# Weights of layer 1's first groups prepared in other steps of a two-layer attention kernel

## What is computed

```python
x = x + tanh(g_xattn[0]) * L0_xattn(layernorm(x), ctx)   # 32 heads of 128, 8 key/value heads, q and k rms-normed
x = x + tanh(g_ffn[0])   * L0_ffn(layernorm(x))          # 8 LoRA experts of rank 16, softmax router
x = x + tanh(g_xattn[1]) * L1_xattn(layernorm(x), ctx)   # 16 heads of 96, 4 key/value heads
x = x + tanh(g_ffn[1])   * L1_ffn(layernorm(x))          # gated, inner width 1792
```

## Time and profile before

| what | us |
|---|---|
| median of 3 runs | 1165.22 |
| lowest and highest | 1164.53, 1165.63 |
| the profiled execution: its time | 1165.63 |
| its span in the trace | 1163.8 |
| PE busy | 1124.8 (97%) |
| DVE busy | 853.7 (73%) |
| ACT busy | 824.6 (71%) |
| mean granted TensorE clock | 0.994 of full speed |

### The profile page before, as it was taken

One profiled execution on the slowest core, in us unless ns is written; L12 is line 12 of the kernel. 1 busy time (PEld: TensorE's weight loads), 2 busy tenths in 40 slices (PEclk: granted clock), 3 DMA queues, 4 the chain that ended last, 5 costly groups with the idle time before them and its releaser, 6 DMA issues.

```text
span 1163.8 us, 22722 instructions
## 1 busy us (share of the span) xinstructions
PE 1124.8 (97%) x7184; PEld 707.8 (61%) x7184; DVE 853.7 (73%) x2066; ACT 824.6 (71%) x2695; POOL 373.6 (32%) x668
## 2 busy tenths in 40 slices
PE   8799999999999999999999999899999999899998
PEld 5456666666666666666656566566666765455554
DVE  5778777667767767677778889898888878743444
ACT  6978888888888888887778867777777765422221
POOL 5754434337533333433345443221111111100000
PEclk8999999999999999999999999999999999999999
DMA  7655654555654656464446566779987795100000
GB/s 255 158 126 113 138 140 120 123 110 110 145 132 91 151 132 139 116 118 106 96 101 139 129 114 131 154 136 186 226 179 138 145 179 103 42 1 1 37 1 37
DMA packets 411992, 139.56 MB, mean 120 GB/s; under 512 B 386656, under 2 KB 396640, under 8 KB 411872
## 3 DMA queue, kind: packets, MB, share of 16 engines
q1 hardware_dynamic: 409968, 134.43, 52.8%
q0 software_dynamic: 1904, 3.67, 1.2%
HBM read 39.21 MB, written 2.10 MB: 35 GB/s over the span
## 4 chain that ended last, share of the span: by engine, by line
PE 77%; DVE 12%; ACT 4%; issue 4%; POOL 3%; DMA 0%; DVEq 0%; POOLq 0%; ACTq 0%
PE bank L541 22%; PE bank L542 21%; PE bank L543 21%; PE bank L740 8%; PE bank L759 4%; DVE pieces L1108 2%; DVE mx L1211 2%; ACT probs L930 1%; DVE stats L1119 1%; POOL rstd L1514 1%; DVE x L1246 1%; DVE q_rows L1108 1%; ACT junk L837 1%; DVE oT L1108 1%; ACT pieces L834 1%
## 5 line engine op out<-in xcount | busy, mean ns | idle before, releaser
L834 ACT ACTIVATE pieces<-probs,rs 128x256 f16<-128x256 f32 x384 | 166.3, 521 | 11.8 <-DVE rs L1226 9.6
L1108 DVE SCALAR_TENSOR_TENSOR pieces<-probs,rs,pieces 128x256 f16<-128x256 f32 x384 | 164.6, 488 | 6.5 <-ACT pieces L834 5.4
L930 ACT ACTIVATE probs<-bank,nb,rq 128x256 f32<-128x256 f32 x256 | 141.3, 564 | 35.3 <-DVE nb L1216 34.9
L1211 DVE TENSOR_REDUCE mx<-bank 128x2 f32<-128x512 f32 x192 | 131.5, 685 | 45.4 <-PE bank L543 45.0
L837 ACT ACTIVATE junk<-bank 128x128 bf16<-128x128 f32 x384 | 101.7, 288 | 55.9 <-PE bank L543 55.9
L541 PE MATMUL bank<-wq,xT 128*128 128x512 f16 (+1 forms) x352 | 127.4, 362 | 3.4 <-DVE q_rows L1108 3.4
L541 PE MATMUL bank<-wo,oT 128*128 128x512 f16 x320 | 121.8, 381 | 6.4 <-DVE oT L1108 4.9
L542 PE MATMUL bank<-wq,xT 128*128 128x512 f16 (+1 forms) x352 | 127.3, 362 | 0.0
L543 PE MATMUL bank<-wq,xT 128*128 128x512 f16 (+1 forms) x352 | 127.1, 361 | 0.0
L543 PE MATMUL bank<-wo,oT 128*128 128x512 f16 x320 | 121.8, 381 | 0.0
L542 PE MATMUL bank<-wo,oT 128*128 128x512 f16 x320 | 121.8, 381 | 0.0
(11 more groups left out here) (216 smaller groups left out, 2841.7 us busy)
## 6 DMA issues: line engine op xcount, KB each, us to landing
raw_o<-in_wo_a SPq DMA_DIRECT2D x8, 1024.0 KB, 6.2
raw_q<-in_wq_a SPq DMA_DIRECT2D x7, 1024.0 KB, 6.1
raw_kv<-in_wkv_a SPq DMA_DIRECT2D x8, 512.0 KB, 3.8
turned<-pieces SPq DMA_TRANSPOSE x192, 2.8
raw_q<-in_wq_c SPq DMA_DIRECT2D x4, 768.0 KB, 4.9
raw_o<-in_wo_c SPq DMA_DIRECT2D x4, 768.0 KB, 5.0
down_rest<-in_down_t POOLq DMA_DIRECT2D x5, 512.0 KB, 4.2
ff_in<-in_gate_t SPq DMA_DIRECT2D x4, 448.0 KB, 4.0
```

What stands on the lines that cost most here:

```text
L834: return act.activation(out, in_, ACT.Copy, scale=scale)
L930: act.activation(probs[:, h, :], bank[h // 2][:, (h % 2) * KV:(h % 2 + 1) * KV], ACT.Exp, bias=nb[:, h:h + 1], scale=scale, accum_out=sums ...
L1108: return dve.scalar_tensor_tensor(out, in_, scale, hi, ALU.mult, ALU.subtract)
L1211: dve.tensor_reduce(mx[:, pr], chunks(bank[i][:, :], 2), AX.X, ALU.max, negate=True).then_inc(mx_done, 1)
```

## The change

Eight rows of three groups join the table of exceptions. Nothing else is changed, and no instruction is added or dropped.

```diff
         ("o", 7): (44, 46, 47, (48, 48, 49, 49)),
+        ("kv", 8): (45, 47, 48, (50, 50)), ("q", 8): (46, 48, 49, (50, 51, 51, 52)), ("o", 8): (50, 52, 53, (54, 55, 56)),
+        ("kv", 9): (58, 64, 65, (66, 67)), ("q", 9): (61, 65, 66, (67, 67, 68, 68)), ("o", 9): (64, 67, 68, (69, 70, 71)),
+        ("kv", 10): (68, 70, 71, (72, 73)), ("q", 10): (70, 71, 72, (73, 74, 75, 76)),
```

## The result

| | before | after |
|---|---|---|
| median of 12 runs each (us) | 1164.43 | 1168.78 |
| lowest and highest | 1162.02, 1167.16 | 1167.17, 1171.36 |
| span of the profiled execution | 1163.8 | 1168.0 |
| mean granted TensorE clock | 0.994 | 0.992 |

The changed kernel takes 1.0038 of the time before, with an interval of 1.0031 to 1.0046: slower by 0.4%, more than the 0.2% that can be told from no change. The forecast was 1167.5 us, and 2.3 us slower than before; it became 4.3 us slower, inside the range of 1162.0 to 1171.0. The forecast lay on the bound of 2.3 us; the measured change lies clear of it.

What follows compares the result with a forecast made beforehand. PE was taken to bound the kernel, with DVE setting the pace in the LoRA stretch. A 3.9 us gain from DVE's relief and a 6.2 us loss from the late q load gave 1167.5 us, range 1162.0 to 1171.0.

Steps and rivals of the forecast that it cites:

- Chunks out of steps 57 to 65: Ten q, o and kv chunks leave these DVE steps: 5.7 us less for DVE between two row maxima.
- the 4 us named as a sign: Sign of being right: PE's waits from 647 us to group 8's end shrink by about 4 us.
- Chunks into 50 to 52 and 54 to 56: Chunks added to DVE: 0.5 us late entering the LoRA tiles, and 0.9 us charged in full in 54 to 56.
- The squares in ACT's steps 47 and 48: Squares moved into these ACT steps have cover from free time and are costed at nothing.
- Steps 66 to 68: Exchanged chunks give DVE 0.9 us more; half counted, 0.4 us. Gain up to step 70: 3.9 us.
- The q load in step 70: Group 10's late load: ACT stands 8 us, PE 4.5 us, slower clock costs 1.7 us; loss 6.2 us.
- The kv load of group 10: Load moves from step 66 to 68, squares from 68 to 70: costs nothing, at most 0.5 us.
- The sum: Profiled 1165.63 - 3.9 + 6.2 = 1167.9 us; median 1165.22 + 2.3 = 1167.5 us.
- SP falls behind: Rival: after ACT's wait SP starts step 71's last transposes too late; loss 8, gain 3, 1170.2 us; chance 0.18.
- A load that isn't felt: Rival: the late q load causes no PE wait in step 72, leaving DVE's relief, 1161.3 us; chance 0.10.
- All idle time gone: Rival: DVE's relief removes all 6.7 us of PE's idle time in the LoRA stretch, 1164.7 us; chance 0.12.

Runs made afterwards that it cites:

- The stand-ins: Kernels with each DMA transpose replaced by two plain DMAs of half its size: the kernel before so edited 1164.42 us, the changed kernel 1168.34 us.
- the load back in step 69: Changed kernel with plain DMAs for transposes, and group 10's q load returned from step 70 to 69: 1163.28 us.
- The run with later squares: Changed kernel with plain DMAs for transposes, q load still in step 70, its squares moved from step 71 to 72: 1162.76 us.
- the stand-in of the change: Changed kernel with each DMA transpose replaced by two plain DMAs of half its size: 1168.34 us.
- the load alone: Kernel before, with plain DMAs for transposes and only group 10's q load moved to step 70: 1173.33 us.

## Why the prediction was right, and where it was not

**Chunks out of steps 57 to 65** (5.7 us). Right, a little large. DVE's stretch shrank by 5.0 us, and DVE did set the pace for most of it. Near the end it no longer does: two waits for PE's scores (0.4 us together) now stand in its list. PE's waits from 647 us to the end of the stretch shrink from 6.7 to 3.8 us, by 2.9 and not by the 4 us named as a sign, while PE gets through the steps from the scores of 58 to those of 68 in 104.5 us in place of 108.8. Where the rest of these 4.3 us comes from, the list of waits doesn't show. That it was DVE's relief is read from the traces; no run took these chunks alone.

**Chunks into 50 to 52 and 54 to 56** (0.5 and 0.9 us). Right. From the scores of 50 to those of 59 the changed kernel loses 1.0 us, for 1.4 us in these two terms. The squares in ACT's steps 47 and 48 cost nothing, as their cover said.

**Steps 66 to 68** (0.4 us) and the sum of the gain. From the scores of 59 to 71 it wins 4.7 us, less 1.0: 3.7 us at step 70, for a forecast of 3.9.

**The q load in step 70** (ACT 8 us, PE 4.5 us, clock 1.7 us). The mechanism is the one forecast, step for step: ACT waits 7.7 us on `raw_q`, PE 4.49 us on `kn`, and the clock falls. SP didn't keep to the forecast's hour, since it too came sooner: the load is issued at 790.1 and not 793.8. PE came sooner by the same measure, so that the distance, and with it the wait, stayed. The term that was mis-sized is the clock: 5.6 us at the lower level, 2.8 us lost, for a forecast of 3.4 and 1.7. I had taken the price from one other wait of the same kernel. So this loss was 7.3 us, and not 6.2: this is the step of the sum whose size was most off.

The landing took 4.9 us from issue, as against the 5.2 us in the sum. The Trainium skill, page DMA: Bandwidth & Descriptors, section Anatomy of one DMA — SWDGE (gpsimd) path, fits about 2.0 us plus the bytes at 436 GB/s to DMAs that GpSimd issues; by that, 768 KB would land in 3.8 us, an estimate. This load is issued by SP, so the fit isn't for it, and no run here issues it from GpSimd; the measured landings of 4.9 and 5.2 us count.

**The kv load of group 10** (nothing, at most 0.5 us). Right: its squares, at 779.13 us, have no wait on the DMA.

**The sum.** On the profiled executions: -0.6 of offset, -3.7 + 7.4, and 0.9 us in the 20 steps after, which the sum didn't have: 4.0 us at the scores of 94. The 0.6 us in the step from the scores of 80 are a wait of PE for the moved probabilities, 1.1 us long, where before it had one of 0.8 without a named releaser. The forecast had 2.3 us for the whole program. The difference is 1.1 us of clock and 0.9 us of these late steps, less the offset, and the gain 0.2 smaller.

**What the sum says of its parts.** Here the forecast seems to have failed, and the net result, whose large terms were each met in place, doesn't show it. It took the two parts as independent: without the late load one should keep 3.9 us. The stand-ins say otherwise. Without the late load 1.1 us is left of 3.4 (1.4 by the ratios, good to some 1.7), and the late load costs 5.1 us in the changed kernel and 8.9 in the kernel before. A step that I never costed, PE coming nearer to SP's queue than SP can follow, seems to stand in their traces, in steps 71 to 81. The changed kernel shows it too: SP stands 6.2 us in step 71, waiting for `k_rows`, and then sets the chain from 807.86 to 865.47 us, until PE waits 1.07 us for the moved probabilities. There it costs only the 0.6 us named above. So the rival "SP falls behind" was right about the changed kernel in kind, SP behind after ACT's wait, and too dear: it had 1.8 us more loss than the forecast. What it didn't have is the load back in step 69, where ACT doesn't wait and part of the gain goes all the same.

**The rivals.** A load that isn't felt: excluded by PE's wait of 4.49 us; the landing came at 795.0, with ACT, DVE and PE all standing for it. The run with later squares shows what it would have given, about no change, and not the 1161.3 us forecast for it. All idle time gone: no, 3.5 us of PE's idle time remain in the stage from 699 us.

What stays open: whether SP's queue takes the gain back; how much of the gain is kept without the late load, more closely than to some 1.7 us; what group 8's rows win without group 9's; and whether the clock alone, without the wait, costs what its rows say.

## What to carry to other kernels

When a load moves past a block of other issues of its queue, ask whether its consumer has to move with it: look at the distance from issue to the first instruction that needs the data, at what that instruction blocks on its engine, and only then at what the move wins. One step more between them was worth 5.6 us here. And follow a gain to the end of the program before it is counted: it lasts only as far as the next engine or queue without slack, here apparently the one that issues the DMAs, which no busy share on the page shows. The chain by engine does show it: 5% for SP's queue where there was none.

## What was not expected of the hardware

The price of a wait in TensorE's clock differs though the waits are alike. After 4.49 us of standing PE worked 5.6 us at 1.2 GHz (2.8 us lost). In the stand-in of the change, after 5.1 us, the stretches show this (us, PE, PEld, DVE, ACT, POOL, clock, DMA share, GB/s):

```profile
796.00:797.00 1.00, 0.00 (x0) 0.00 (x0) 0.00 (x0) 0.67 (x1) 0.00 (x0) 0.76 0.87 309
...
803.00:804.00 1.00, 1.00 (x12) 0.92 (x10) 1.00 (x3) 1.00 (x3) 0.00 (x0) 0.82 0.59 133
```

PE starts again at 799.63 us and the full clock is back at 803.4, so it works 3.8 us at the lower level (1.9 us lost). There the clock had fallen 3.1 us before PE went on, and in the changed kernel 1.2 us before. With the load alone it fell 1.5 us before PE went on after 4.90 us, and PE worked 5.3 us at the lower level (2.7 us lost). Among these three the earlier the clock fell within the wait, the less of PE's work it slowed. It isn't a rule: in the wait of 3.43 us that the forecast took its price from, the clock was at 0.81 in the stretch from 43 to 44 us, so it fell just as PE went on, and only 3.4 us of work were slowed.

Two plain DMAs of half the size, in rows of 256 bytes, took the place of each DMA transpose on a queue that is nearly full (SP's waits from 755 to 885 us add up to 0.5 us) without moving the time: 1164.42 us beside 1163.68, an interval of 0.9994 to 1.0016.
